# GNN kernel: counts added by two engines from bases in order of use, rank products and sums interleaved, first small loads issued by ScalarE

## The chip, the cores and the metric

The kernel runs on one core of one Trainium2 chip. The metric is the device time of one execution in microseconds (us), the median of several runs.

## What is computed

Two graph networks run one after the other on 3125 nodes with 128 features and 103125 edges, sorted by target node. The first is a four-layer GCN; the second has three relational layers over 16 edge types. For each (target, type) pair the second needs the number of edges, by which its sums are divided. Cut to that:

```python
seg = tgt * R + edge_type
agg = segment_sum(x[src], seg, N * R).reshape(N, R, d)
cnt = segment_sum(ones_like(edge_type), seg, N * R).reshape(N, R, 1)
out = einsum('nrd,rdo->no', agg / clip(cnt, 1.0), W_r) + x @ root_r + bias_r
```

## The kernel before, in words

The program is a row of stages. In each, every engine has a list of instructions written out by hand, ordered by semaphores, and a barrier of all engines ends it. A wait stands in front of one instruction; the instructions queued behind it on the engine wait too. Seven stages run in this order: `prepare`, `slots`, `count_relations`, `inverses_and_norm`, `build_adjacency`, `gcn_layers`, `relations`. The stages after the first two have a second, general form that runs only if the input breaks an assumption of the fast form (a flag decides); the inputs here take the fast form throughout.

`prepare` (from L217): SyncE (SP) issues 13 loads on one semaphore, `s_ld`: sources, targets and types of all edges (L230 to L232, 128x816 words each), the first target of each group of 512 edges (`gbase`, L233), and nine small ones (L235 to L237): three gains and three shifts of 256 words and three scalars, each broadcast to 128 partitions. VectorE and ScalarE wait for all 13. VectorE (L254 to L300) then forms `dloc`, the place of each edge's target within its group's window of 19 nodes; only L278 and L279 read the gains. A reciprocal (L300) ends it.

`slots` (from L1893): the rank of each edge among those of its group and block of sources. TensorE writes 24 sums into six PSUM banks in turn (L2028 to L2031), and VectorE picks from each: a product with a one-hot (L1972, 128x500 into one of two buffers `sized`) and a sum over blocks (L1974) that reads it. After the product stands a wait for its end and an `sem_inc` (L1973), which TensorE needs before it writes the bank again. 20 of the 24 steps are 500 wide, 4 are 25 wide.

`count_relations` (from L445): 202 groups of 512 edges, four at a time in 51 rounds. VectorE copies types and places to float16 (L485, L486), ScalarE fills the unused half of one one-hot (L517, eight instructions), VectorE makes the one-hots (L492 and L494, 70 instructions in two parts), and TensorE multiplies them (L533, four matmuls a round), which leaves a 128x76 result whose four diagonal blocks of 16x19 are the counts of four groups. Six rounds share a PSUM bank. VectorE then adds each block into `t.quarters` at the group's base node (L508): 202 additions of 16x19, one after another. The base comes from a register; 12 registers are loaded at a time (L499, the first 12 at L488), and each addition waits for the fourth one before it, which added to the same quarter of `t.quarters`. The first addition of every four has two waits, one for the bank (L505) and behind it the one for the fourth addition before (L507). The same form, two waits in a row ahead of one VectorE instruction, stands in the next stage at L630 and L631, ahead of L632. The four quarters are summed by a matmul in the next stage.

## Time and profile before

| | us |
|---|---|
| median of 3 runs | 3432.25 (3431.44 to 3438.33) |
| profiled execution | 3401.57 |
| its span | 3399.8 |
| TensorE busy | 2653.2 (78%) |
| VectorE busy | 2193.1 (65%) |
| ScalarE busy | 1323.8 (39%) |
| GpSimd busy | 1219.4 (36%) |

The profiled execution is 30.7 us shorter than the median of the unprofiled ones. Times in the rows are from the span's start, in us. In a row of the timeline, the start comes first, then the duration (of several instructions together where it ends in "x" and a number), then engine, line, operation, what is written and read; square brackets hold the idle time of the engine before it and what ended it. A "q" behind an engine's name means its sequencer.

### The profile page before, as it was taken

To read this page: it belongs to the slowest core of one execution; us is meant where nothing else is said; L and a number is where in the kernel's file an instruction comes from. 1 tells how busy PE (TensorE), PEld (TensorE's weight loads), DVE (VectorE), ACT (ScalarE), POOL (GpSimd) and SP (SyncE) were. 2 spreads that over 40 slices of the span, in tenths; PEclk is the share of its full clock that TensorE was granted. 3 is DMA by queue.
4 is the path that set the end of the run, shared out by engine and by line. 5 is a ranking of instruction groups with operands and counts; after the bars stand their busy time and mean duration, and the time that the engine had idled before them with its cause. 6 is when DMAs were issued, how large, how long until landed. Compare 5 with 4: busy or idle time off the path is not lost.

```text
span 3399.8 us, 80962 instructions
## 1 busy us (share of the span) xinstructions
PE 2653.2 (78%) x24551; PEld 1772.8 (52%) x24552; DVE 2193.1 (65%) x7930; ACT 1323.8 (39%) x2937; POOL 1219.4 (36%) x1269
## 2 busy tenths in 40 slices
PE   3337777768899995888888888888888888888887
PEld 1323333335456683555555555555555555555555
DVE  6689999976453454666566556656666556566665
ACT  0149999973222212333333333333333333333332
POOL 3020000000000002555555545555555455555554
PEclk9569999999999997999999999999999999999999
DMA  0011111121101026444444444444444444454442
GB/s 26 20 58 43 46 43 46 43 68 47 32 24 45 8 78 208 121 124 122 121 118 121 124 123 118 121 122 123 120 120 122 124 119 122 121 123 121 120 121 80
DMA packets 228329, 314.99 MB, mean 93 GB/s; under 512 B 41665, under 2 KB 201004, under 8 KB 227708
## 3 DMA queue, kind: packets, MB, share of 16 engines
q1 hardware_dynamic: 187548, 227.23, 24.9%
q0 software_dynamic: 40672, 86.39, 9.0%
q8 instruction: 58, 0.95, 0.1%
q14 instruction: 51, 0.42, 0.0%
HBM read 268.23 MB, written 45.23 MB: 92 GB/s over the span
## 4 chain that ended last, share of the span: by engine, by line
PE 25%; DMA 16%; issue 10%; POOL 3%; DVE 3%; another core or an unknown queue 3%; DVEq 0%; POOLq 0%; ACT 0%; SPq 0%; ACTq 0%
DMA arena<-pair,arena 15%; PE psum L2308 8%; PE psum L2321 7%; PE psum L2332 4%; PE psum L2285 4%; POOL arena L2218 3%; DVE arena L2501 1%; PE psum L2298 1%; DVE arena L2507 1%; DVE arena L2497 1%; DVE arena L2537 0%; DMA arena<-rows 0%; PE psum L2386 0%; DMA pair<-arena 0%
## 5 line engine op out<-in xcount | busy, mean ns | idle before, releaser
L2218 POOL DMA_INDIRECT arena<-pair,arena x1212 | 1161.1, 958 | 906.7 <-DMA h<-h 381.9
L2507 DVE SCALAR_TENSOR_TENSOR arena<-psum,arena,work 128x304 f32<-128x304 f32 x606 | 429.9, 710 | 718.7 <-DMA h<-h 469.5
L2442 ACT ACTIVATE arena<-psum 128x512 f16<-128x512 f32 x303 | 180.7, 597 | 1108.3 <-remote 763.1
L2321 PE MATMUL psum<-arena 128*128 128x304 f16 x3939 | 566.1, 293 | 18.9 <-issue 17.8
L2308 PE MATMUL psum<-arena 128*128 128x304 f16 x2424 | 370.6, 296 | 207.3 <-DMA arena<-pair,arena 162.2
L2501 DVE TENSOR_SCALAR arena<-arena 128x304 f16<-128x304 f16 x2121 | 483.1, 300 | 0.0
L2321 PEld LDWEIGHTS psum<-arena 128*128 128x128 f16 x3939 | 360.9, 98 | 193.5 <-issue 81.7
L2285 PE MATMUL psum<-arena 128*32 128x256 f16 x7272 | 367.1, 277 | 117.9 <-issue 109.1
L2439 ACT ACTIVATE arena<-psum 128x1024 f16<-128x1024 f32 x303 | 308.9, 1019 | 227.8 <-DMA h<-h 134.7
L2308 PEld LDWEIGHTS psum<-arena 128*128 128x128 f16 x2424 | 213.7, 98 | 346.7 <-issue 234.4
L2332 PE MATMUL psum<-arena 128*128 128x152 f32 (+1 forms) x2496 | 378.0, 297 | 6.5 <-DVE arena L2507 6.5
L1254 PE MATMUL psum<-arena,h 128*128 128x512 f16 x1250 | 346.6, 383 | 19.4 <-DMA h<-h 19.4
L2332 PEld LDWEIGHTS psum<-arena 128*128 128x128 f32 x2496 | 346.1, 194 | 20.6 <-DVE arena L2507 10.0
L2285 PEld LDWEIGHTS psum<-arena 128*32 128x32 f16 x7272 | 157.4, 95 | 282.2 <-issue 264.4
L2497 DVE TENSOR_SCALAR arena<-arena 128x304 f16<-128x304 f16 x1212 | 280.2, 295 | 27.3 <-ACT arena L2420 19.0
L1062 POOL DMA_DIRECT2D h<-h x9 | 8.3, 926 | 799.4 <-issue 538.6
L1255 PE MATMUL psum<-arena,h 128*128 128x128 f16 x1250 | 275.3, 220 | 0.0
L989 PE MATMUL psum<-h,work 128*128 128x512 f16 (+1 forms) x404 | 110.6, 356 | 145.8 <-DVE work L853 145.8
L931 ACT ACTIVATE work<-h 128x128 f16<-128x128 f16 x707 | 216.6, 395 | 0.1
L1254 PEld LDWEIGHTS psum<-arena,h 128*128 128x128 f16 x1250 | 123.3, 99 | 168.3 <-DMA h<-h 20.2
L2537 DVE TENSOR_TENSOR arena<-arena,psum 128x19 f32 x606 | 105.8, 175 | 98.2 <-PE psum L2332 16.3
L2445 ACT ACTIVATE arena<-psum 64x128 f16<-64x128 f32 x606 | 159.7, 264 | 7.4
(289 smaller groups left out, 3217.6 us busy)
## 6 DMA issues: line engine op xcount, KB each, us to landing
work<-inverse SPq DMA_DIRECT2D x606, 152.0 KB
arena<-pull SPq DMA_DIRECT2D x303, 224.0 KB
pull<-rows SPq DMA_DIRECT2D x101, 224.0 KB
arena<-pair,arena POOLq DMA_INDIRECT x1212
h<-work SPq DMA_DIRECT2D x8, 640.0 KB
h<-h POOLq DMA_DIRECT2D x8, 640.0 KB, 6.9
pair<-arena SPq DMA_DIRECT2D x12, 256.0 KB
x_pad<-arena SPq DMA_DIRECT2D x1, 1600.0 KB, 5.3
```

Of the source, the lines that this page charges most:

```text
L931: e.activation(t.away[:, k, :], t.iota_h[:, 0:P], ACT.Abs, bias=t.stage[:, par, 0, k:k + 1], scale=-1.0).then_inc(s_df, 1)
L1254: e.matmul(bank[:, at:at + 512], wt, adj[:, b, i * GN:i * GN + 512], start=a, stop=z)
L1255: m = e.matmul(bank[:, at + 512:at + GN], wt, adj[:, b, i * GN + 512:i * GN + GN], start=a, stop=z)
L2218: e.indirect_dma_start(out=t.msg[:, j, k].rearrange("p h f -> p (h f)"), out_offset=None, in_=d[f"pair_{l}"].rearrange("n h f -> n (h f)") ...
L2285: m = e.matmul(p.psum[CAP * (b % 4):CAP * (b % 4) + CAP, GATHER + c // 2, c % 2 * 2 * RF:(c % 2 + 1) * 2 * RF], t.pull[:, slot, b * CAP:(b ...
L2308: m = e.matmul(p.psum[:, 0, 0:KEYS], t.msg[:, j % TP, tile, half, :], t.oh[:, j % 2, tile, :], start=(tile == 0 and half == 0), stop=(tile ...
L2321: m = e.matmul(p.psum[:, 1, 0:KEYS], t.smsg[:, j % 2, tile, half, :], t.soh[:, j % 2, tile, :], start=(tile == 0 and half == 0), stop=(til ...
L2332: m = e.matmul(p.psum[:, OUT + h, 0:n], t.wr[:, r, :], t.agg[h][:, r, :, :].rearrange("p g w -> p (g w)")[:, 0:n], start=(r == 0), stop=(r ...
L2439: e.activation(t.smsg[:, q, 0:4].rearrange("p k h f -> p (k h f)"), p.psum[:, GATHER:GATHER + 2, :].rearrange("p b n -> p (b n)"), ACT.Cop ...
L2497: e.tensor_scalar(t.oh[:, j % 2, k, :], t.iota[:, 0:KEYS], t.keys[:, j * GT + k:j * GT + k + 1], None, ALU.is_equal).then_inc(s_oh, 1)
L2501: e.tensor_scalar(t.soh[:, j % 2, c, :], t.iota[:, 0:KEYS], t.skeys[:, at:at + 1], None, ALU.is_equal).then_inc(s_oh, 1)
L2507: e.scalar_tensor_tensor(t.agg[h % 2][:, :, k % BATCH, :], p.psum[:, k % 2, 0:KEYS].rearrange("p (r w) -> p r w", r=REL), t.back[:, l:l + ...
```

## The change

Three things are changed. In `prepare` ScalarE issues the nine small loads, on a semaphore of their own (`s_gn`); VectorE waits at its start for the other four only, and for the nine in front of L278. In `slots` the products and sums of successive steps are interleaved: product n+1 is issued ahead of sum n, with a wait for sum n-1, and the product itself counts up the semaphore for TensorE. In `count_relations` VectorE adds only the blocks of the first two quarters (102 of them); ScalarE copies the blocks of the other two from PSUM to SBUF as float16, one bank at a time (18 copies), and GpSimd adds those (100 additions). The bases are first put into `t.bases` in the order in which each engine uses them, by two copies. In the general forms, a buffer `nodes_0` takes the place of `rows_0`.

```diff
@@ -231,11 +231,8 @@
         e.dma_start(t.gbase, d["gbase"].partition_broadcast(P)).then_inc(s_ld, 16)
-        for k in range(3):
-            e.dma_start(t.gains[:, k], d[f"g{k}"].partition_broadcast(P)).then_inc(s_ld, 16)
-            e.dma_start(t.gains[:, 3 + k], d[f"beta{k}"].partition_broadcast(P)).then_inc(s_ld, 16)
-            e.dma_start(t.sig[:, k:k + 1], d[f"a{k}"].partition_broadcast(P)).then_inc(s_ld, 16)
-        e.wait_ge(s_ld, 13 * 16)
+        e.wait_ge(s_ld, 4 * 16)
+        e.wait_ge(s_gn, 9 * 16)
...
@@ -250,7 +247,7 @@
         v = Tally(p.sem("prep"))
-        e.wait_ge(s_ld, 13 * 16)
+        e.wait_ge(s_ld, 4 * 16)
         v.inc(e.tensor_copy(t.typf, t.typ))
...
@@ -275,6 +272,7 @@
                               ALU.subtract))
+        e.wait_ge(s_gn, 9 * 16)
         v.inc(e.tensor_reduce(t.red[:, 3:4], t.gains[:, 0:3], AX.XY, ALU.max, apply_absolute_value=True))
...
@@ -301,7 +299,11 @@
     def _(e):
-        e.wait_ge(s_ld, 13 * 16)
+        for k in range(3):
+            e.dma_start(t.gains[:, k], d[f"g{k}"].partition_broadcast(P)).then_inc(s_gn, 16)
+            e.dma_start(t.gains[:, 3 + k], d[f"beta{k}"].partition_broadcast(P)).then_inc(s_gn, 16)
+            e.dma_start(t.sig[:, k:k + 1], d[f"a{k}"].partition_broadcast(P)).then_inc(s_gn, 16)
+        e.wait_ge(s_gn, 9 * 16)
         e.wait_ge(s_sq, 1)
...
@@ -464,6 +468,12 @@
         return a.rearrange("p (m g k) -> p m g k", g=G, k=GT)
+
+    def load(e, regs, part, q):
+        first, stop = part * 2 * LOAD, min(GPAD, (part + 1) * 2 * LOAD)
+        if first < NG:
+            e.load(regs[part % 2][0:(stop - first) // 2],
+                   t.bases[0:1, q // 2 * (GPAD // 2) + first // 2:q // 2 * (GPAD // 2) + stop // 2])
...
@@ -478,6 +488,25 @@
         e.memset(t.x[:, BLOCKS - 1, :], 0.0).then_inc(s_tail, 1)
+        e.wait_ge(s_tail, 1)
+        regs = [[e.alloc_register(f"copy_base{q}_{k}") for k in range(LOAD)] for q in range(2)]
+        e.wait_ge(s_16, 4)
+        load(e, regs, 0, 2)
+        done = 0
+        for n in range(NG):
+            if n % (2 * LOAD) == 0:
+                load(e, regs, n // (2 * LOAD) + 1, 2)
+            m, q = n // G, n % G
+            if q < 2:
+                continue
+            base = e.snap(regs[n // (2 * LOAD) % 2][n % (2 * LOAD) // G * 2 + q - 2], min_val=0, max_val=NODES - 1)
+            to = t.quarters[32 * q:32 * q + REL, bass.ds(base, RWIN)]
+            if m % PER_BANK == 0:
+                e.wait_ge(s_cp, 2 * (m // PER_BANK) + q - 1)
+            if done > 1:
+                e.wait_ge(s_ag, done - 1)
+            e.tensor_tensor(to, to, t.copies[32 * q:32 * q + REL, m * RWIN:(m + 1) * RWIN], ALU.add).then_inc(s_ag, 1)
+            done += 1
...
@@ -485,28 +514,34 @@
         typ, dloc = (a.rearrange("p (g n) -> p g n", g=G) for a in (t.typ16, t.dloc16))
-        e.load(regs[0], t.gbase[0:1, 0:LOAD])
-        e.wait_ge(s_16, 2)
+        for h in range(2):
+            e.tensor_copy(t.bases[0:1, h * (GPAD // 2):(h + 1) * (GPAD // 2)].rearrange("p (m g) -> p m g", g=2),
+                          t.gbase[0:1, :].rearrange("p (m g) -> p m g", g=G)[:, :, 2 * h:2 * h + 2]).then_inc(s_16, 1)
+        e.wait_ge(s_16, 4)
+        load(e, regs, 0, 0)
         for a, z in PARTS:
             for r in range(REL):
                 e.tensor_scalar(t.hot_r[:, :, r, a:z], typ[:, :, a:z], float(r), None, ALU.is_equal)
             for w in range(RWIN):
                 one = e.tensor_scalar(t.hot_c[:, :, w, a:z], dloc[:, :, a:z], float(w), None, ALU.is_equal)
             one.then_inc(s_hot, 1)
+        done = 0
         for n in range(NG):
-            if n % LOAD == 0 and n + LOAD < NG:
-                more = min(LOAD, NG - n - LOAD)
-                e.load(regs[n // LOAD % 2 ^ 1][0:more], t.gbase[0:1, n + LOAD:n + LOAD + more])
+            if n % (2 * LOAD) == 0:
+                load(e, regs, n // (2 * LOAD) + 1, 0)
             m, q = n // G, n % G
+            if q > 1:
+                continue
             bank, at = place(m)
-            base = e.snap(regs[n // LOAD % 2][n % LOAD], min_val=0, max_val=NODES - 1)
+            base = e.snap(regs[n // (2 * LOAD) % 2][n % (2 * LOAD) // G * 2 + q], min_val=0, max_val=NODES - 1)
             to = t.quarters[32 * q:32 * q + REL, bass.ds(base, RWIN)]
             if q == 0:
                 e.wait_ge(s_mm, min(ROUNDS, (m // PER_BANK + 1) * PER_BANK))
-            if n >= G:
-                e.wait_ge(s_ad, n - G + 1)
+            if done > 1:
+                e.wait_ge(s_ad, done - 1)
             e.tensor_tensor(to, to, p.psum[32 * q:32 * q + REL, bank, at + q * RWIN:at + (q + 1) * RWIN],
                             ALU.add).then_inc(s_ad, 1)
+            done += 1
...
@@ -516,6 +551,13 @@
                              ACT.Copy).then_inc(s_rest, 1)
+        for h in range(BANKS):
+            m0, m1 = h * PER_BANK, min(NG // G, (h + 1) * PER_BANK)
+            e.wait_ge(s_mm, m1)
+            for q in (2, 3):
+                sums = p.psum[32 * q:32 * q + REL, h % 8, 0:(m1 - m0) * WIDE].rearrange("p (m w) -> p m w", w=WIDE)
+                e.activation(t.copies[32 * q:32 * q + REL, m0 * RWIN:m1 * RWIN].rearrange("p (m w) -> p m w", w=RWIN),
+                             sums[:, :, q * RWIN:(q + 1) * RWIN], ACT.Copy).then_inc(s_cp, 1)
...
@@ -528,7 +570,8 @@
             if m >= 8 * PER_BANK:
-                e.wait_ge(s_ad, PER_BANK * G)
+                e.wait_ge(s_ad, PER_BANK * 2)
+                e.wait_ge(s_cp, 2)
             for k in range(GT):
...
@@ -1198,7 +1241,7 @@
-                e.dma_start(d["rows_0"][:, cols].rearrange("p (b f) -> p b f", f=RF), ex).then_inc(s_st, 16)
+                e.dma_start(d["nodes_0"][rows].rearrange("(b p) f -> p b f", p=P), ex).then_inc(s_st, 16)
...
@@ -1658,7 +1701,7 @@
-        e.dma_start(t.hrows, d["rows_0"].rearrange("p (b f) -> p b f", f=RF)).then_inc(s_r, 16)
+        e.dma_start(t.hrows, d["nodes_0"].rearrange("(b p) f -> p b f", p=P)).then_inc(s_r, 16)
...
@@ -1699,7 +1742,7 @@
-                 out=t.msg[:, 0, :], out_offset=None, in_=p.d[f"rows_{l}"][:, :],
+                 out=t.msg[:, 0, :], out_offset=None, in_=p.d[f"rows_{l}" if l else "nodes_0"][:, :],
...
@@ -1963,16 +2006,29 @@
-        n = 0
-        for q, g0, g1 in SPREAD:
-            for k in range(GT):
-                e.wait_ge(s_rk, n + 1)
-                w = (g1 - g0) * BLOCKS
-                x = t.sized[n % 2][:, 0:w]
-                v.link(e, e.tensor_tensor(x, p.psum[:, n % 6, 0:w], flat(t.ohb[:, k, g0:g1, :]), ALU.mult))
-                e.sem_inc(s_used)
-                v.inc(e.tensor_reduce(grid(t.place)[:, g0:g1, k], x.rearrange("p (g b) -> p g b", b=BLOCKS), AX.X, ALU.add))
-                n += 1
+        steps = [(g0, g1, k) for q, g0, g1 in SPREAD for k in range(GT)]
+
+        def chosen(n):
+            g0, g1, k = steps[n]
+            w = (g1 - g0) * BLOCKS
+            e.wait_ge(s_rk, n + 1)
+            if n > 1:
+                e.wait_ge(s_sum, n - 1)
+            e.tensor_tensor(t.sized[n % 2][:, 0:w], p.psum[:, n % 6, 0:w], flat(t.ohb[:, k, g0:g1, :]),
+                            ALU.mult).then_inc(s_used, 1)
+
+        def summed(n):
+            g0, g1, k = steps[n]
+            e.wait_ge(s_used, n + 1)
+            e.tensor_reduce(grid(t.place)[:, g0:g1, k],
+                            t.sized[n % 2][:, 0:(g1 - g0) * BLOCKS].rearrange("p (g b) -> p g b", b=BLOCKS),
+                            AX.X, ALU.add).then_inc(s_sum, 1)
+
+        chosen(0)
+        for n in range(len(steps)):
+            if n + 1 < len(steps):
+                chosen(n + 1)
+            summed(n)
...
@@ -1983,6 +2039,7 @@
+        e.wait_ge(s_sum, len(steps))
...
@@ -2591,6 +2648,8 @@
+    t.copies = p.work[:, GPAD + NPAD + TPAD:GPAD + NPAD + TPAD + 25 * RWIN].bitcast(F16)
+    t.bases = p.work[:, GPAD + NPAD + TPAD + 25 * RWIN:2 * GPAD + NPAD + TPAD + 25 * RWIN].bitcast(I32)
...
@@ -2632,6 +2691,7 @@
+    make("nodes_0", (NPAD, RF), F32)
     make("table_0", (P, BLOCKS * 2 * RF), F16)
```

## Rows read from the trace of the kernel before

**Rows 1.** By stretch: busy us of PE, PEld, DVE, ACT, POOL; clock, DMA share, GB/s

```profile
103.00:138.00 35.00, 28.52 (x204) 28.17 (x204) 25.00 (x145) 10.84 (x8) 0.00 (x0) 0.50 0.16 46
138.00:177.00 39.00, 0.00 (x0) 0.00 (x0) 21.86 (x128) 0.00 (x0) 0.00 (x0) 0.50 0.00 1
```

**Rows 2.** Timeline of the count stage: matmuls, additions, and what follows

```profile
109.22 28.52 PE L533 MATMUL psum<-arena 128*128 128x76 f16 x204 [21.86 <-DVE arena L494]
...
115.30 2.39 DVE L508 TENSOR_TENSOR work<-work,psum 16x19 f32 x12
...
148.92 2.69 DVE L508 TENSOR_TENSOR work<-work,psum 16x19 f32 x12 [0.99 <-DVE work L508]
...
171.91 5.04 DVE L508 TENSOR_TENSOR work<-work,psum 16x19 f32 x22 [1.22 <-issue]
```

**Rows 3.** Sequencer instructions by line: duration ns min/median/max, first and last start

```profile
L499 DVEq TENSOR_LOAD <-work x16: 846/848/1086, 113.3 to 170.5; - x16
...
L507 DVEq EVENT_SEMAPHORE  x50: 21/21/21, 115.5 to 176.4; - x50
...
L631 DVEq EVENT_SEMAPHORE  x5: 21/21/21, 199.8 to 203.6; - x5
```

**Rows 4.** ScalarE in the count stage, and its smallest common copy from PSUM

```profile
102.09 11.75 ACT L517 ACTIVATE arena<-work 128x1600 f16<-128x1600 f16 x8 [77.23 <-DVE work L485]
...
L2445 ACT ACTIVATE arena<-psum 64x128 f16<-64x128 f32 x606 | 159.7, 264 | 7.4
```

**Rows 5.** GpSimd's instructions grouped by shape: busy us, mean ns of one | idle before

```profile
L2218 POOL DMA_INDIRECT arena<-pair,arena x1212 | 1161.1, 958 | 906.7 <-DMA h<-h 381.9 <-issue 325.9 <-PE psum L2321 149.5
...
L1914 POOL TENSOR_SCALAR_AFFINE_SELECT arena<-arena 125x125 f16<-125x125 f16 x2 | 0.6, 334 | 0.1
L1916 POOL TENSOR_SCALAR_AFFINE_SELECT arena<-arena 125x5 f16<-125x5 f16 x1 | 0.5, 504 | 0.0
...
L247 POOL TENSOR_SCALAR_AFFINE_SELECT ident<-ident 128x128 f32<-128x128 f32 x1 | 0.3, 292 | 0.2 <-POOL ident L245 0.2
...
L245 POOL MEMSET ident<- 128x128 f32 x1 | 0.2, 194 | 0.0
...
L2663 POOL MEMSET const-float32-1.0<- 128x1 f32 x1 | 0.1, 102 | 0.0
```

**Rows 6.** Timeline from 27 us: GpSimd beside a VectorE product of two SBUF inputs

```profile
27.34 11.16 DVE L1929 TENSOR_TENSOR arena<-arena 128x2525 f16<-128x2525 f32 x4 [1.99 <-issue]
...
30.25 2.83 POOL L1905 TENSOR_SCALAR_AFFINE_SELECT arena<-arena 125x125 f16<-125x125 f16 x1
```

**Rows 7.** Timeline of the first 25 us: issue of the loads, VectorE's work

```profile
2.21 0.43 SPq L233 DMA_DIRECT2D work<-in_gbase  x1
...
6.50 1.15 SPq L237 DMA_DIRECT2D arena<-in_a  x1
13.01 0.58 DVE L254 CAST arena<-arena 128x816 f32<-128x816 int32 x1 [12.89 <-DMA arena<-in_a]
...
20.41 0.95 DVE L278 TENSOR_REDUCE arena<-arena 128x1 f32<-128x768 f32 x1
```

**Rows 8.** DMA issues of the first 14 us, size, median us to landing

```profile
arena<-in_g SPq DMA_DIRECT2D x3, 128.0 KB, 6.4
...
work<-in_gbase SPq DMA_DIRECT2D x1, 102.0 KB, 4.4
```

**Rows 9.** Busy time by stretch in the first microseconds, columns as in rows 1

```profile
4.00:5.00 1.00, 0.00 (x0) 0.00 (x0) 0.00 (x0) 0.00 (x0) 0.00 (x0) 1.00 1.05 385
6.00:7.00 1.00, 0.00 (x0) 0.00 (x0) 0.00 (x0) 0.00 (x0) 0.00 (x0) 1.00 1.06 238
```

**Rows 10.** Timeline of VectorE in the rank steps: product, sum, next product

```profile
62.34 0.68 DVE L1972 TENSOR_TENSOR arena<-psum,arena 128x500 f32<-128x500 f32 x1
63.16 0.68 DVE L1974 TENSOR_REDUCE arena<-arena 128x20 f32<-128x500 f32 x1
63.75 0.67 DVE L1972 TENSOR_TENSOR arena<-psum,arena 128x500 f32<-128x500 f32 x1
```

6 lines of the change are left out of this document (4 added, 2 removed).

## The prediction

> **What bounds the kernel now.** The change touches the first 177 us of a span of 3399.8. I read the busy times by stretch first. From 138 to 177 us VectorE alone works, 21.86 us busy of 39; TensorE, ScalarE and GpSimd do nothing; while the matmuls run, GpSimd is idle too and TensorE's granted clock is 0.50, its lower level of 1.2 GHz [rows 1]. Then the timeline: the 204 matmuls are over 28.52 us after 109.22, but the 202 additions run from 115.30 to 176.95 [rows 2], and the barrier follows. So the additions set the end of this stage, with some 39 us in which nothing else runs. Twelve additions take 2.69 us and are followed by 0.99 us of idle time [rows 2]; what fills it is the load of 12 registers, 848 ns on VectorE's sequencer [rows 3]. In the first stage the timeline shows VectorE at rest until 13.01 us, released by the last small load, issued at 6.50; the last of the four large ones was issued at 2.21 [rows 7] and landed 4.4 us later [rows 8]. In the rank steps VectorE is never long idle: product at 62.34, sum at 63.16, next product at 63.75, thus 1.41 us a step [rows 10]. All three stages hang on VectorE, and a barrier ends each, so what they lose in length, the program loses. Later stages get the same work later or earlier as a whole.
>
> **First loads.** The nine small loads leave SP's queue and are issued by ScalarE, idle until then. By itself, `gbase` lands at 2.21 + 4.4 = 6.6 us [rows 7, 8], and VectorE could start at 6.8. But now the small loads (six of 128 KB, 0.77 MB) run beside the large ones. At 385 and 238 GB/s, what the DMA engines moved at 4 and 6 us [rows 9], all of it costs 2.0 to 3.2 us, none of it 0; I take half of it at 238 GB/s, 1.6 us, since ScalarE issues the last ones when the large ones have mostly landed. Start at 8.3, thus 13.01 - 8.3 = 4.7 us saved. Ends: 6.2 (start at 6.8) and 1.5 (start at 11.5, if the new queue slows the old one more than bytes explain; a small load now takes 6.4 us to land where 102 KB took 4.4 [rows 8]). The moved wait stands in front of L278, which VectorE reaches 20.41 - 13.01 = 7.4 us after its start [rows 7], at 15.7; even the landing of today, 13.0, is earlier, so it costs nothing.
>
> **Rank steps.** It looks as if two stalls a step were taken away. They are not. Product n+1 waits for sum n-1, and that sum stands directly ahead of it on the same queue; it must, since there are only two buffers. Before, the sum waited for the product just ahead of it; after, the product waits for the sum just ahead of it: one stall a step as before, 63.16 - (62.34 + 0.68) = 0.14 us [rows 10]. Its size stays as well. Today an `sem_inc` instruction stands in that gap. It goes, but the product has two waits now, and where an instruction has two waits, the trace shows the second as an instruction of its own: L631 is the second wait ahead of L632, and L507 shows one in front of every first addition of a four [rows 3]. The second wait is the one for the sum, so the same instruction fills the same gap. I take 0; the ends are 24 x 0.14 = 3.4 us gained if the gap goes altogether, and 24 x 0.02 (the 21 ns of one more sequencer instruction [rows 3]) = 0.5 us lost.
>
> **Start of the count stage.** Two copies of 102 bases are added, and the first load of registers, which ran beside L485, now waits for both and stands ahead of the one-hots. 0.2 us each for the copies, an estimate above the 0.17 of an addition [rows 2], plus 0.85 for the load [rows 3]: 1.25 us on VectorE, all of it in front of the one-hots. They, the matmuls and the additions move from 115.30 to 116.55.
>
> **VectorE's additions.** Two of four stay: 102. An addition takes 2.69/12 = 0.22 us [rows 2]; now every second one, not every fourth, has a second wait, so I take 0.25. Eight loads of registers stay of 16, at 0.92 us each (period of twelve, 2.69 + 0.99 = 3.68 [rows 2], less twelve starts 0.23 apart). 102 x 0.25 + 8 x 0.92 = 32.9: VectorE ends at 149.4. TensorE keeps ahead: a round takes 28.52/51 = 0.56 us [rows 2], two additions and their share of the loads 0.64.
>
> **GpSimd's additions.** They start when ScalarE is through L517, at 102.09 + 11.75 = 113.84 [rows 4], TensorE has filled the first bank (109.22 + 1.25 + 6 x 0.56 = 113.8) and two copies are made, at 0.264 us each as the nearest row [rows 4]: about 114.3. The copies of the later banks, 18 x 0.26 = 4.8 us in all, lie beside the matmuls on an engine that is idle. The price of one addition decides all; the trace has no two-input operation on GpSimd. Lower end: 0.10, a memset of one column. Upper end: 0.504, the dearest undisturbed select, 125x5. Between: a memset of 128x128 takes 0.194, the select that also reads it 0.292 [rows 5], so one read costs 0.10; a small memset and two reads give 0.10 + 2 x 0.10 = 0.30. I take 0.30. With eight loads of registers at VectorE's 0.92 (7.4 us; GpSimd has its own bases), it ends at 114.3 + 30 + 7.4 = 151.7. That is later than VectorE's 149.4, so GpSimd sets the end of the stage: 176.95 - 151.7 = 25.2 us saved. If it were cheaper, VectorE would be the bound: 27.5.
>
> The Trainium skill speaks against the move: its page GPSIMD Engine Reference, section Performance versus the Vector engine, has GpSimd at about half of VectorE's speed in two-input elementwise work. By it an addition would cost 2 x 0.17 = 0.34 (an estimate from that ratio), the stage would end at 155.7 and the kernel at 3406. No row here has such an operation on GpSimd.
>
> **Rest.** `nodes_0` is touched by the general forms only, which these inputs don't run: 0.
>
> **Sum.** 4.7 + 0 + 25.2 = 29.9 us (the 1.25 is within the 25.2). The profiled execution would go from 3401.57 to 3371.6. It lies 30.7 below the median of the runs; nothing in the change bears on that distance, so the median goes from 3432.25 to 3402.3.
>
> **Rivals.**
> (a) The two adders get in each other's way. For it: a select of 125x125 on GpSimd took 2.83 us beside VectorE products of 2.79 us with two SBUF inputs [rows 6], against 0.334 alone [rows 5]. Against it: VectorE's addition has one input in PSUM. The Trainium skill (SBUF — State Buffer, Who interferes with whom) names just this difference: it sees contention with two SBUF inputs, none with one; the first half agrees with the 2.83 us, the second is seen in no row. If they took turns, a pair would cost 0.17 + 0.30 = 0.47 on both: 116.55 + 102 x 0.47 + 7.4 = 171.9, 5.0 us saved there, 9.7 in all: 3422.5.
> (b) GpSimd is dear: each addition costs what its DMA instructions cost, 0.958 [rows 5], because each goes through software and waits for the end of the one before the last. It would end at 114.3 + 95.8 + 7.4 = 217.5, 40.6 later than now; less 4.7, the kernel is 35.9 slower: 3468. The sum is zero at (181.65 - 121.7)/100 = 0.60 us an addition and slower by more than 0.2% from 0.67. Against it: all plain GpSimd operations of small size undisturbed by VectorE are at or below 0.504 [rows 5].
> (c) GpSimd at 0.54 to 0.67 an addition: the gain of the loads and the loss of the additions cancel within 7 us: 3432.
> (d) The start does not do what it says: both queues slow each other, and VectorE starts at 11.5: 3405.5.
>
> **How the numbers follow.** Forecast (additions at 0.10 to 0.40, first load gain of 3 to 6) 0.64; (d) 0.09; (a) 0.16; (c) 0.05; (b) 0.06. What this kernel's measurement can tell from no change is about 0.2%, 6.9 us. The range: below, VectorE sets the end (27.5), start 6.2, rank gap gone 3.4: 3395, and 4 for the scatter of the runs: 3391. Above, an addition at 0.504 (end 172.1, 4.8 saved) with 1.5 at the start: 3426. It takes in the forecast, (d) and (a). Faster 0.89, same 0.05, slower 0.06.
>
> **What would show it.** In the profile after: first copy of VectorE at 7 to 9 us; in the rank steps still 1.4 us a step, with a gap now behind the sum and none behind the product; one-hots starting 1.2 us later in the stage; 102 additions on VectorE over 33 us; 100 on GpSimd with 0.3 from start to start, ending 2 us behind VectorE's. Wrong if GpSimd's additions are more than 0.45 apart, or VectorE's own get longer beside them, or the next stage's start does not move with the additions.

## The result and the profile after

| | before | after |
|---|---|---|
| median of 6 runs | 3433.16 (3431.44 to 3438.33) | 3420.65 (3418.87 to 3425.55) |
| ratio, 95% interval | | 0.9965 [0.9955, 0.9975] |
| profiled execution | 3401.57 | 3420.5 |
| its span | 3399.8 | 3418.8 |

The median of before is over three executions more than in the table ahead of the prediction. The change saves 12.5 us, by the interval 8.6 to 15.4. The forecast was 29.9 us. The direction held, and the time is inside the range; less than half of the gain arrived.

The two spans can't be compared as wholes. The last stage took 2097.0 us in the profiled execution of before and 2126.9 in that of after, although nothing in it was changed; in later profiles of kernels that leave it alone it took 1862 to 1879 us on some chips and 2125 to 2131 on others. So from here on stages are compared, from barrier to barrier. The first four lie ahead of everything that varies:

| stage, us | before | after | difference | forecast |
|---|---|---|---|---|
| first loads (`prepare`) | 26.2 | 23.7 | -2.5 | -4.7 |
| rank steps (`slots`) | 74.0 | 72.6 | -1.4 | 0 |
| counts (`count_relations`) | 77.9 | 64.5 | -13.4 | -25.2 |
| normalization (`inverses_and_norm`) | 30.7 | 38.3 | +7.6 | 0 |
| end of the four | 208.8 | 199.1 | -9.7 | -29.9 |

The next two stages are within 1.1 us of before. The two terms of the sum came in at about half of their size, and a stage that the change doesn't touch pays 7.6 us.

Read by stretch (columns as in [rows 1]; count stage and normalization of after), GpSimd now works 24 us of the count stage, and VectorE's busy time in the normalization stage is 31.5 us where it is 23.88 before:

```profile
96.30:160.80 64.50, 28.47 (x204) 28.13 (x204) 31.44 (x176) 16.24 (x26) 24.01 (x101) 0.50 0.10 26
160.80:199.10 38.30, 10.85 (x50) 10.74 (x50) 31.48 (x95) 5.21 (x7) 15.15 (x11) 0.50 0.33 103
```

TensorE's granted clock is 0.50 in both stages, its lower level of 1.2 GHz, as in [rows 1]; the clock plays no part in the difference.

The timeline of the count stage of after, which answers to [rows 2] (start, duration, engine, line):

```profile
98.96 0.40 DVE L518 COPY work<-work 1x102 int32<-1x102 int32 x2
102.24 2.86 DVE L524 TENSOR_SCALAR arena<-work 128x400 f16<-128x400 f16 x16 [2.88 <-issue]
...
112.48 5.45 POOL L508 TENSOR_TENSOR work<-work 16x19 f16 x12 [15.27 <-ACT work L559]
...
115.48 2.84 DVE L542 TENSOR_TENSOR work<-work,psum 16x19 f32 x12 [0.87 <-PE psum L576]
...
150.69 2.88 DVE L542 TENSOR_TENSOR work<-work,psum 16x19 f32 x12 [2.88 <-issue]
...
155.45 4.60 POOL L508 TENSOR_TENSOR work<-work 16x19 f16 x16 [1.26 <-issue]
```

and by line, sequencer instructions among them, for the loads of registers (which answer to the L499 of [rows 3]) and both kinds of additions:

```profile
L475 DVEq TENSOR_LOAD <-work x9: 1406/2723/2782, 99.4 to 153.4; - x9
L475 POOLq TENSOR_LOAD <-work x9: 1386/2706/2721, 99.5 to 153.8; - x9
...
L508 POOL TENSOR_TENSOR work<-work x100: 212/218/2209, 112.5 to 159.8; 16x19 f16 x100
...
L542 DVE TENSOR_TENSOR work<-work,psum x102: 160/166/171, 115.5 to 159.7; 16x19 f32 x102
```

The additions are what they were forecast to be: 0.218 us each on GpSimd, 0.293 from start to start (forecast 0.30); 0.166 on VectorE, 0.216 and 0.284 from start to start in turn, 0.26 in the mean (0.25). The loads are not. The same instruction with the same 12 registers takes 2.72 us where it took 0.848, on both engines. The gaps "2.88 <-issue" ahead of the one-hots and ahead of additions are these loads.

The normalization stage of after, VectorE and GpSimd:

```profile
167.08 11.04 POOL L610 MEMSET arena<- 128x1600 f32 x8
...
169.70 8.46 DVE L654 TENSOR_SCALAR arena<-arena 128x25 f32<-128x25 f32 x1
178.19 0.18 DVE L656 TENSOR_SCALAR arena<-psum 128x25 f32<-128x25 f32 x1
```

In the kernel before, the same instruction (there L611), on the same data, among the same eleven memsets:

```profile
183.05 12.45 POOL L567 MEMSET arena<- 128x1600 f32 x9
...
187.04 0.22 DVE L611 TENSOR_SCALAR arena<-arena 128x25 f32<-128x25 f32 x1
190.28 0.18 DVE L613 TENSOR_SCALAR arena<-psum 128x25 f32<-128x25 f32 x1 [3.01 <-PE psum L649]
```

VectorE would have waited 3.0 us for TensorE there in any case, so an instruction of 8.46 us instead of 0.22 delays what follows by 8.24 - 3.0 = 5.2 us, of which experiments 6 to 8 find 4.6 at the stage's end. That is not all of the 7.6: the rest is at the end of the stage. VectorE's last branch there, and the DRAIN behind it:

```profile
L169 DVEq COMPARE_BRANCH  x1: 69/69/69, 194.0 to 194.0; - x1
...
L173 DVEq DRAIN  x1: 41/41/41, 198.2 to 198.2; - x1
```

Between the two lie 4.08 us in which VectorE does nothing; before, the same two stand at 206.7 and 207.3, and SP came to the barrier last, at 207.9. Here SP came at 195.2 and VectorE last.

In the first stage, the two queues issue side by side (answers to [rows 7]):

```profile
1.75 0.43 SPq L232 DMA_DIRECT2D arena<-in_typ_pt  x1
...
2.19 1.55 ACTq L303 DMA_DIRECT2D arena<-in_g  x1
2.23 1.54 SPq L233 DMA_DIRECT2D work<-in_gbase  x1
...
10.44 0.58 DVE L251 CAST arena<-arena 128x816 f32<-128x816 int32 x1 [10.31 <-DMA work<-in_gbase]
```

### The profile page after: what moved, and what is told of

Same layout as the page of the kernel before. It is cut to its first block, busy times and chain, and to the rows that moved or that the text cites. A ratio compares the mean times of both kernels' runs of the same rounds, so it can differ in the third digit from the quotient of the medians.

```text
span 3418.8 us, 81004 instructions
## 1 busy us (share of the span) xinstructions
PE 2676.5 (78%) x24551; PEld 1778.2 (52%) x24552; DVE 2179.1 (64%) x7832; ACT 1328.0 (39%) x2955; POOL 1247.5 (36%) x1369
## 4 chain that ended last, share of the span: by engine, by line
PE 28%; DMA 11%; issue 10%; DVE 5%; another core or an unknown queue 4%; POOL 2%; DVEq 0%; ACT 0%; POOLq 0%; SPq 0%; ACTq 0%
DMA arena<-pair,arena 11%; PE psum L2378 8%; PE psum L2365 8%; PE psum L2389 5%; PE psum L2342 5%; DVE arena L2558 2%; POOL arena L2275 2%; PE psum L2355 1%; DVE arena L2554 1%; DVE arena L2564 1%; DVE arena L2594 0%; DMA arena<-rows 0%; PE psum L2443 0%; DVEq L2594 0%
## 5 line engine op out<-in xcount | busy, mean ns | idle before, releaser
L2342 PE MATMUL psum<-arena 128*32 128x256 f16 x7272 | 400.8, 277 | 199.3 <-issue 186.5
L2342 PEld LDWEIGHTS psum<-arena 128*32 128x32 f16 x7272 | 166.3, 94 | 390.2 <-issue 368.2
L2389 PEld LDWEIGHTS psum<-arena 128*128 128x128 f32 x2496 | 341.4, 191 | 13.9 <-DVE arena L2564 3.1
```

The costliest lines, as they stand in the source:

```text
L2342: m = e.matmul(p.psum[CAP * (b % 4):CAP * (b % 4) + CAP, GATHER + c // 2, c % 2 * 2 * RF:(c % 2 + 1) * 2 * RF], t.pull[:, slot, b * CAP:(b ...
L2389: m = e.matmul(p.psum[:, OUT + h, 0:n], t.wr[:, r, :], t.agg[h][:, r, :, :].rearrange("p g w -> p (g w)")[:, 0:n], start=(r == 0), stop=(r ...
```

## The experiments

Ratios are to the kernel before on the same chip. Some chips take some 250 us less for the last stage, so times of different experiments aren't compared with each other. Where only one execution was made, the reading rests on the lengths of stages, and no ratio is given: where nothing in them was changed, the slots, count and normalization stages repeat within 0.2 us from chip to chip, the first stage within 1 us. Line numbers in a fence are those of the kernel it is of.

**1. Where the bases lie: `start_aligned`.** The copied bases started at word 4695 of `work` (a word is 4 bytes), those for GpSimd at 4797; the original bases, read in 0.848 us, at word 0. One edit moves the start to 4696:

```diff
-    t.bases = p.work[:, GPAD + NPAD + TPAD + 25 * RWIN:2 * GPAD + NPAD + TPAD + 25 * RWIN].bitcast(I32)
+    t.bases = p.work[:, GPAD + NPAD + TPAD + 476:2 * GPAD + NPAD + TPAD + 476].bitcast(I32)
```

> The changed kernel, with the array of bases moved by one word, from word 4695 to 4696 of the scratch row; its second half, read by GpSimd, stays 102 words on, at 4798. Theory (where the words lie): a load of 12 registers takes four adjacent words in one read where they start at a multiple of four, and one word a read otherwise. VectorE's loads (4696 + 12k, multiples of four) fall from 2.72 to 0.85 us; GpSimd's (4798 + 12k, never) stay at 2.7. VectorE's additions then end about 8 x 1.87 = 14 us earlier, but GpSimd's still end the stage, so the kernel gains at most the 1.9 us of the first load ahead of the one-hots. Rival (two engines loading at once, or words just written by a copy, make loads slow): both stay at 2.7 us, as the same engines load the same copied words.

Measured, loads by line:

```profile
L475 DVEq TENSOR_LOAD <-work x9: 834/848/868, 99.6 to 139.4; - x9
L475 POOLq TENSOR_LOAD <-work x9: 1390/2708/2758, 99.6 to 152.2; - x9
```

VectorE's half, now at a multiple of four words, is fast; GpSimd's, at 4798, is slow. VectorE's additions end at 145.3, GpSimd's at 158.5, and the stage is 62.7 us long instead of 64.5: GpSimd alone holds its end.

**2. Both halves at a multiple of four: `both_aligned`.**

```diff
-                   t.bases[0:1, q // 2 * (GPAD // 2) + first // 2:q // 2 * (GPAD // 2) + stop // 2])
+                   t.bases[0:1, q // 2 * 104 + first // 2:q // 2 * 104 + stop // 2])
```

(and the copies and the tile's size to match).

> As the kernel before this one, and the second half too starts at a multiple of four (word 4800, halves 104 apart). Theory of the words' place: loads of both engines at 0.75 to 0.85 us; VectorE's additions span 31 us instead of 44.4, GpSimd's 34 to 35 instead of 47.6, the one-hots start 1.9 earlier, the count stage lasts 64.5 - 15 = 49 to 50 us, and the kernel gains 14 to 16 us on the changed one: about 3405. Rival theory: no change, 3420.

Measured: 3155.31 (3145.71 to 3161.09), before 3183.98 on that chip; ratio 0.9916 [0.9903, 0.9929], where the change alone gave 0.9965. Loads and additions:

```profile
L475 DVEq TENSOR_LOAD <-work x9: 834/850/867, 99.5 to 139.4; - x9
L475 POOLq TENSOR_LOAD <-work x9: 795/808/835, 99.6 to 140.6; - x9
...
141.72 4.60 POOL L508 TENSOR_TENSOR work<-work 16x19 f16 x16 [0.67 <-POOL work L508]
```

The count stage takes 50.6 us, 13.9 less than in after and 27.3 less than before. VectorE's 102 additions take 32.5 us from first to last (forecast 32.9), GpSimd's 100 take 35.6 (forecast 37.4), and GpSimd ends 1.1 us behind VectorE (0.2 us in after). With fast loads the forecast for this stage would have been too low by 2 us and not too high by 12.

**3. The same without the rest of the change: `odd_before` and `even_before`.** The kernel before, its bases copied to word 4695 (odd), or to 4694 (even, but no multiple of four), and loaded from there:

```diff
-        e.load(regs[0], t.gbase[0:1, 0:LOAD])
-        e.wait_ge(s_16, 2)
+        e.tensor_copy(t.odd[0:1, :], t.gbase[0:1, :]).then_inc(s_16, 1)
+        e.wait_ge(s_16, 3)
+        e.load(regs[0], t.odd[0:1, 0:LOAD])
```

> The kernel before, with one added copy of the 204 bases to an odd word (4695) and the registers loaded from there; all 202 additions stay on VectorE, GpSimd adds nothing. Theory of the words' place: all 17 loads at 2.7 us instead of 0.85; 16 of them between additions, 16 x 1.87 = 30 us longer, and 2.3 more for the copy and the first load ahead of the one-hots: about 32 us slower than the kernel before. Rival (two engines loading at once): loads stay at 0.85, at most 1.3 us slower.

> The kernel before with its 204 bases copied to a word that is even but no multiple of four (4694), from where the registers are loaded, 12 at a time. The bases' own place is a multiple of four words (a load of 12 takes 0.85 us), the copy to 4695 took 2.73 us a load. Theory (only a start at a multiple of four words, 16 bytes, is fast): 2.7 us a load, count stage 109.6 as with the odd word. Rival (a multiple of two words, 8 bytes, is enough, or gives half): 0.85 to 1.6 us a load, count stage 78.5 to 91.

Measured from the odd word:

```profile
L500 DVEq TENSOR_LOAD <-work x16: 2285/2722/2727, 116.4 to 201.2; - x16
```

From the even word the median is 2722 ns as well. Both are slow, and the count stage takes 109.6 us in both. `odd_before` is 28.6 us slower than before, ratio 1.0091 [1.0076, 1.0106] (3212.62 us). So neither the second engine nor the interleaved order of the bases matters; the place does, and a multiple of two words isn't enough. The count stage lost 31.7 us, and the whole 28.6, with an interval of 24 to 34. What a load costs per register: 2.72/12 = 0.227 us from an unfit place, and 1.406/6 = 0.234 for the last, short one; 0.848/12 = 0.071 from a fit one. This looks like one read of 0.23 to 0.28 us for each four registers in the one case and for each register in the other; the 10 registers of before's last load, from a fit place, took 1.086 [rows 3], which two reads of four and two single ones would give (four reads at 0.27). The last load of `both_aligned` on VectorE, 6 registers from a fit place, took 0.834: as long as 12, as one read of four and two single ones would. A load with 4 or 8 registers was not run. And the place isn't all there is: the load of one register that begins each later stage, always from the same word, took 0.31 us in most stages, 0.55 at 26.3 and 0.94 at 208.9 in before. What sets that, no run shows.

**4. The first loads: `prepare_alone` and `prepare_one_queue`.** The first puts the change's own first part into the kernel before. The second leaves the issues where they were, on SP behind the large ones, and moves only the semaphore and the wait:

```diff
-            e.dma_start(t.gains[:, k], d[f"g{k}"].partition_broadcast(P)).then_inc(s_ld, 16)
+            e.dma_start(t.gains[:, k], d[f"g{k}"].partition_broadcast(P)).then_inc(s_gn, 16)
...
-        e.wait_ge(s_ld, 13 * 16)
+        e.wait_ge(s_ld, 4 * 16)
+        e.wait_ge(s_gn, 9 * 16)
```

> The kernel before with the first-stage part of the change alone: ScalarE issues the nine small loads. The prediction's step: first copy of VectorE at 8.3, 4.7 us earlier. What the changed kernel's profile says: 10.4, 2.6 earlier, since the two queues' issues slow each other. Expected: first copy at 10.4 +- 0.2, the issues of SP at 1.0 to 1.6 us each instead of 0.43, first stage 23.7 us instead of 26.2, later stages as before, normalization at 30.7.

> The kernel before with the small loads still issued by SP behind the four large ones, but counted on a semaphore of their own, so that VectorE waits for the four large ones alone and for the small ones only where it reads them (the wait ahead of L278). No second queue issues. Theory (what cost 2.1 of the forecast 4.7 us is the second queue's issuing, not its bytes): SP's issues stay at 0.43, gbase is issued at 2.2 and lands at 6.6, first copy at 6.8 to 7.5; the small loads land at 13.0 as before, ahead of the wait at some 14.5, so the first stage is 5.5 to 6 us shorter than before (20.3 to 20.8). Rival (the small loads' bytes behind the large ones delay them): first copy at 9 or later.

Measured for `prepare_alone`: first copy at 10.19, stage 23.4 us, the others as before. The expectation of 1.0 to 1.6 us for every issue of SP was wrong: only the last of its four is slow, 1.52 us, the three ahead of it took 0.42 to 0.43. For `prepare_one_queue`, the timeline:

```profile
2.21 0.43 SPq L233 DMA_DIRECT2D work<-in_gbase  x1
...
6.57 1.35 SPq L237 DMA_DIRECT2D arena<-in_a  x1
6.97 0.58 DVE L255 CAST arena<-arena 128x816 f32<-128x816 int32 x1 [6.85 <-DMA work<-in_gbase]
```

First copy at 6.97, stage 20.2 us: 6.0 less than before, without a second queue. The times from issue to landing (median) tell where the changed kernel loses it. First its rows, then those of `prepare_one_queue`:

```profile
arena<-in_src_pt SPq DMA_DIRECT2D x1, 408.0 KB, 5.1
...
work<-in_gbase SPq DMA_DIRECT2D x1, 102.0 KB, 8.2
```

```profile
arena<-in_src_pt SPq DMA_DIRECT2D x1, 408.0 KB, 3.3
...
work<-in_gbase SPq DMA_DIRECT2D x1, 102.0 KB, 4.7
```

With the second queue the base loads need 8.2 us instead of 4.7, 3.5 more, of which 1.54 - 0.43 = 1.1 is the issue itself and 2.4 comes after it. Already the very first load, issued at 0.8 us beside ScalarE's first, lands 1.8 us later. So the theory of the expectation (issuing, not bytes) covers a third. The larger part comes in the transfers; that the large and the small ones now share the DMA engines from the start would explain it, but no run separates this from other effects of the second queue. With one queue the small ones follow, and nothing waits for them: they had landed when SP's wait ended at 12.84, and VectorE is at the place that needs them some 14 us into the stage.

**5. The stall of the rank steps: `rank_three_buffers`.** The kernel before with the change's interleaving and three buffers:

```diff
-    t.sized = [c(ACROSS * BLOCKS) for _ in range(2)]
+    t.sized = [c(ACROSS * BLOCKS) for _ in range(3)]
...
+            if n > 2:
+                e.wait_ge(s_sum, n - 2)
```

> The kernel before with the interleaved rank steps of the change, but with three buffers for the products in turn instead of two, and the product waiting for the sum but two ahead of it. The prediction's step: with two buffers one stall a step is left, because the product waits for the sum that stands directly ahead of it. With three, both waits are for instructions that lie one instruction back. Expected: 0.14 to 0.2 us a step less than before (1.41), period 1.2 to 1.27, the slots stage 3.5 to 5 us shorter than the 74.0 of before, where two buffers gave 1.4. Rival (the step is bound by the two engines' work, 0.68 + 0.59, and not by the stall): period 1.36 as with two buffers.

Measured: the slots stage takes 68.3 us, 5.7 less than before. The timeline, first of after (two buffers), then of this kernel:

```profile
61.73 0.68 DVE L2017 TENSOR_TENSOR arena<-psum,arena 128x500 f32<-128x500 f32 x1
62.32 0.67 DVE L2023 TENSOR_REDUCE arena<-arena 128x20 f32<-128x500 f32 x1
63.09 0.68 DVE L2017 TENSOR_TENSOR arena<-psum,arena 128x500 f32<-128x500 f32 x1
```

```profile
63.48 0.66 DVE L1980 TENSOR_REDUCE arena<-arena 128x20 f32<-128x500 f32 x1
64.06 0.67 DVE L1974 TENSOR_TENSOR arena<-psum,arena 128x500 f32<-128x500 f32 x1
64.64 0.66 DVE L1980 TENSOR_REDUCE arena<-arena 128x20 f32<-128x500 f32 x1
```

A step takes 63.09 - 61.73 = 1.36 us with two buffers and 64.64 - 63.48 = 1.16 with three. With three, each instruction starts 0.58 us after the one before it, although each takes 0.67: where the next one doesn't wait for the end of the last, the two overlap by 0.09. So a wait for the instruction directly ahead costs the gap of 0.10 and this overlap, about 0.2 a step.

**6. VectorE held by the memsets: `no_port_wait`, `held_later`.** The first writes the same value with another instruction:

```diff
-        v.inc(e.tensor_scalar(n.value[:, BLOCKS:], n.mv[:, :, 1], EPS, None, ALU.add))
+        v.inc(e.scalar_tensor_tensor(n.value[:, BLOCKS:], n.mv[:, :, 1], EPS, n.mv[:, :, 1], ALU.add, ALU.max))
```

> The changed kernel, in which the one VectorE instruction in the next stage that took 8.46 us beside GpSimd's memsets (var + eps as a tensor_scalar) is a scalar_tensor_tensor with the same result, max(var + eps, var), from two SBUF inputs. Theory (a form of VectorE instruction that takes the SBUF interface shared with GpSimd was held until GpSimd's row of memsets was over): the new form is not held, takes 0.2 us, the stage lasts 30.4 us instead of 38.1, and the kernel gains 7.6 us: about 3413. Rival (any VectorE instruction is held there, or the unprofiled runs have no such hold): no gain in the runs.

Measured: 3168.21 (3164.67 to 3172.9), ratio 0.9952 [0.994, 0.9964]; normalization stage 33.5 us. Timeline:

```profile
169.83 0.19 DVE L654 SCALAR_TENSOR_TENSOR arena<-arena 128x25 f32<-128x25 f32 x1
173.06 0.18 DVE L656 TENSOR_SCALAR arena<-psum 128x25 f32<-128x25 f32 x1 [3.05 <-PE psum L692]
```

Nothing is held; 4.8 of the 7.6 us come back and 2.8 do not. The second puts five small instructions of this kind ahead of the TENSOR_SCALAR, which stays:

```diff
+        for k in range(5):
+            e.wait_ge(v.sem, v.n)
+            v.inc(e.scalar_tensor_tensor(n.tmp[:, 5 * k:5 * k + 5], n.mv[:, 0:5, 1], EPS, n.mv[:, 0:5, 1], ALU.add, ALU.max))
```

> The changed kernel with five small scalar_tensor_tensor instructions (into a scratch tile) ahead of the TENSOR_SCALAR of the variances, which starts some 0.7 to 1 us later by them. In the changed kernel it starts at 169.70, 0.13 us before the next of GpSimd's eleven memsets starts, and takes 8.46 us, until the last memset ends; in the kernel before it stands at the same distance and takes 0.22. Theory (VectorE's instruction is held whenever it meets GpSimd's row of queued memsets, until the row ends): it now takes 7.5 to 7.8 us and still ends at 178.1. Rival (it is a tie of one moment, at which the next memset gets ahead of VectorE; elsewhere it is held for the memset that runs at most): it takes 0.2 to 1.4 us and the normalization stage is 33.5 to 35 us instead of 38.3.

Measured:

```profile
170.78 7.49 DVE L657 TENSOR_SCALAR arena<-arena 128x25 f32<-128x25 f32 x1
178.30 0.18 DVE L659 TENSOR_SCALAR arena<-psum 128x25 f32<-128x25 f32 x1
```

1.08 us later it is held 0.97 less and ends at the same place, when the last of the eleven memsets ends. The rival, a tie of one moment, falls. That the five instructions ahead of it were not held beside the same memsets agrees with `no_port_wait`.

**7. What brings the hold about: `one_add_before`, `one_load_before`.** The hold came with every kernel that had the new count stage and this TENSOR_SCALAR, and with none that had the old stage. In the kernel before, one addition on GpSimd is put into the count stage, for nothing, or else one load of 12 registers:

```diff
+        e.memset(t.other, 0.0).then_inc(s_one, 1)
+        e.wait_ge(s_one, 1)
+        e.tensor_tensor(t.other[:, 0:RWIN], t.other[:, RWIN:2 * RWIN], t.other[:, 0:RWIN], ALU.add).then_inc(s_one, 1)
```

> The kernel before with one two-input addition on GpSimd (16x19, SBUF only, into a scratch tile, behind a memset of it) at the start of the count stage, where GpSimd is idle for the rest of the stage. In all kernels with the changed count stage, GpSimd's eleven memsets of the next stage have a step of 1.367 us at first, last 1.42 from the third on, and VectorE's TENSOR_SCALAR is held until the last of them ends (8.46 us; started 1.08 later it was held 7.49 and ended at the same memset). In all kernels with the count stage of before, the memsets' step is 1.374, and the same TENSOR_SCALAR takes 0.22. Theory (GpSimd keeps what its additions left it in, and so takes the port for a whole row): with one such addition the hold appears, 8.4 us, and the normalization stage takes 35 us instead of 30.7. Rival (it is the moment at which the stage starts, or something else in the count stage): 0.22 us, 30.7.

> The kernel before with one load of 12 registers on GpSimd in the count stage and no addition there. Theory of the addition: no hold, TENSOR_SCALAR 0.22 us, normalization stage 30.7. Rival (reading registers from SBUF is what changes GpSimd's memsets): hold of 8.4 us, stage 35.

Measured with the addition:

```profile
101.20 0.21 POOL L484 TENSOR_TENSOR work<-work 16x19 f32<-16x19 f32 x1
```

```profile
180.19 15.17 POOL L572 MEMSET arena<- 128x1600 f32 x11 [78.78 <-DVE arena L614]
```

```profile
186.93 8.47 DVE L616 TENSOR_SCALAR arena<-arena 128x25 f32<-128x25 f32 x1
```

One addition of 0.21 us at 101.20, in another stage and 85 us before, and VectorE is held for 8.47 us; the normalization stage takes 35.3 us instead of 30.7. With the register load it takes 30.7, and the TENSOR_SCALAR 0.22.

**8. What ends it: `select_after_adds`, `iota_after_adds`.** The changed kernel, with one instruction of another kind behind GpSimd's last addition. The first (its scratch tile left out):

```diff
+        e.wait_ge(s_ag, done)
+        e.memset(t.other, 0.0).then_inc(s_ag, 1)
+        e.wait_ge(s_ag, done + 1)
+        e.affine_select(out=t.other, in_=t.other, compare_op=ALU.not_equal, fill=1.0, base=0, pattern=[[-1, RWIN]],
+                        channel_multiplier=1).then_inc(s_ag, 1)
```

> The changed kernel with a memset and a select of 128x19 on GpSimd behind its last addition (scratch tile), some 0.5 us in the count stage. One addition on GpSimd, 80 us earlier and in another stage, was enough to have VectorE's TENSOR_SCALAR held for the rest of the row of memsets. In the kernel before, GpSimd ran only iotas, selects and memsets before that place, and nothing was held. Theory (the last instruction of another kind decides how GpSimd's memsets go): behind a select they go as before, the memsets' step is 1.374 from the first on, TENSOR_SCALAR takes 0.2, the normalization stage 33.5 to 34 us (the 3 us at the branch are left). Rival (one addition changes it for good): 8.46 us, 38.3.

> The same with an iota of 128x19 in place of memset and select. Theory as for the select if any instruction but a memset restores the old behaviour: TENSOR_SCALAR 0.2 us, normalization stage 33.5 to 34. Rival (only a select does, or nothing): 8.46 us, 38.3.

Measured with the select, which took 0.20 us at 161.01:

```profile
170.86 0.22 DVE L659 TENSOR_SCALAR arena<-arena 128x25 f32<-128x25 f32 x1
174.09 0.18 DVE L661 TENSOR_SCALAR arena<-psum 128x25 f32<-128x25 f32 x1 [3.01 <-PE psum L697]
```

The hold is gone; with the iota as well (0.222 us). The normalization stage takes 33.7 us in both. So it hangs on which instruction GpSimd ran last, memsets not counted: behind an addition its row of memsets keeps VectorE out to the end, behind a select or an iota it lets VectorE in between two of them. It shows in the memsets too: here and in before the one that VectorE cut in front of takes 1.46 us and the others 1.43; in after none takes longer than 1.43. What in GpSimd differs, no trace shows.

**9. The branch: `code_shifted`.** 64 short memsets and a wait at the head of VectorE's part of the first stage of the changed kernel, where VectorE idles until 10.4 us:

```diff
         v = Tally(p.sem("prep"))
+        for k in range(64):
+            v.inc(e.memset(t.dloc[:, k:k + 1], 1.0))
+        e.wait_ge(v.sem, v.n)
```

> The changed kernel with 64 short memsets (into t.dloc, which is written again later) at the head of VectorE's part of the first stage, where it idles until 10.4 us anyway. It moves all of VectorE's later code by 65 instructions, and nothing else. In the changed kernel VectorE's last instruction of the normalization stage, the branch over the general form (L169) at 194.03, is followed by 4.08 us of nothing, with a block of instructions of 8192 bytes fetched at 196.32 inside it; before, the same gap is 0.47. Theory (the target of the branch is no longer among the instructions at hand, because VectorE's program has become some 300 instructions shorter): with the code moved by half a block the gap is 0.5 and the normalization stage goes from 38.3 to about 34.8 us, or the gap appears behind another branch. Rival (VectorE waits there for something of the stage's work, a store or GpSimd): the gap stays at 4 us, wherever the code lies.

Measured:

```profile
L169 DVEq COMPARE_BRANCH  x1: 69/69/69, 194.1 to 194.1; - x1
...
L173 DVEq DRAIN  x1: 69/69/69, 194.7 to 194.7; - x1
```

The gap is 0.47 us, as before, and the stage takes 35.3 us instead of 38.3; that is 3.0 and not 3.6 less, since SP now comes to the barrier last, at 195.3. Where the code lies decides. Not all of it reaches the end of the kernel: the next stage, `build_adjacency`, took 543.9 us here and 542.9 in after, and 543.3 to 544.9 in all ten profiles without the long gap against 542.3 to 543.4 in the seven with it, 1.3 us in the mean. The packets of an instruction queue fit this. In after, between 194 and 199 us:

```profile
q14 instruction: 2, 0.02, 0.8%
```

that is two blocks of 8192 bytes, of which one starts at 196.32, behind the branch; in `code_shifted` the last one ahead of the branch starts at 185.33, none between it and the DRAIN, and the next at 196.35, behind the barrier. VectorE executes 306 instructions fewer than before up to there, so it looks as if the target of this branch, which skips the general form of the stage, came to lie in a block that isn't fetched yet; for which engine a block is fetched, the profile doesn't say. The Trainium skill (Runtime: NRT & Kernel Launch, Instruction fetch mechanics) describes just this: instructions come in blocks in straight order, and a taken branch out of the blocks at hand stalls for a fetch. The trace agrees, with a block fetched inside a gap of 4.08 us.

**10. All of it together: `all_mended`.** The edits of 2, 4 (one queue), 5, 6 (other instruction) and 9 in the changed kernel, and the first register load behind the one-hots instead of ahead of them.

> The changed kernel with each place mended that the runs so far point to: small loads issued by SP behind the large ones but counted by themselves; three product buffers in the rank steps; the bases copied to words that are a multiple of four, for both halves; the first load of registers behind the one-hots; the variance's addition written as scalar_tensor_tensor (max of var + eps and var, the same value); and VectorE's code moved by 65 instructions with short memsets at its head. Theory (each cause stands by itself, so the stages add up as they did alone): first stage 20.2 to 20.5, slots 68.3, counts 49.5 to 50.6, normalization 30.4 to 31, in all 169 to 171 us instead of 208.8, thus 38 to 40 us and a ratio of 0.9875 +- 0.002. Rival (a later wait takes over in one of them, as the norm stage did in the changed kernel): one of the four stages is more than 1.5 us above these numbers.

Measured: 3132.81 (3131.66 to 3134.46), before 3172.9 on that chip; ratio 0.9872 [0.985, 0.9893], 40.1 us less than before. By stretch (first stage, slots, counts, normalization):

```profile
0.00:21.20 21.20, 0.20 (x2) 0.10 (x3) 12.55 (x96) 1.49 (x2) 1.87 (x8) 1.00 0.35 102
21.20:89.50 68.30, 30.25 (x175) 16.63 (x175) 56.09 (x100) 0.00 (x0) 24.87 (x22) 0.91 0.00 0
89.50:139.30 49.80, 28.47 (x204) 28.13 (x204) 31.38 (x176) 16.26 (x26) 23.44 (x101) 0.50 0.12 34
139.30:170.00 30.70, 10.85 (x50) 10.74 (x50) 23.82 (x95) 5.21 (x7) 15.16 (x11) 0.50 0.36 114
```

170.0 us where before needs 208.8: 38.8 less. Each stage is as long as the mended causes make it one by one, but for two: the first takes 21.2 instead of 20.2, as `gbase` landed 5.7 us after its issue in this execution, not 4.7, and the counts take 49.8 instead of 50.6, with the first load behind the one-hots.

## Why the prediction was right or wrong

**Count stage, the failed step: "Eight loads of registers stay of 16, at 0.92 us each" and, for the first one, "0.85 for the load".** The price was read from the row of the old load [rows 3] and carried to loads from another place, whose address nobody looked at. They took 2.72 us. The copies sit at word 4695, behind a tile of 25 x 19 words. That costs 1.9 us ahead of the one-hots (they start 3.2 us later in the stage, forecast 1.25) and 1.9 for each further load of 12 on GpSimd: 64.5 - 50.6 = 13.9 us in all, by `both_aligned`. This term alone takes the forecast gain from 29.9 to 16.0 us. What else there is in the stage was 2.1 us dearer in the forecast (77.9 - 25.2 = 52.7) than in `both_aligned` (50.6). The Trainium skill (Runtime: NRT & Kernel Launch, Instruction fetch mechanics) gives about 200 ns per register for a load of registers, even in bulk; it speaks of loads from HBM, and these come from SBUF. The 0.227 us from an unfit place are near that figure, the 0.071 from a multiple of four words are not, and the measurement decides.

**Additions: right.** 0.293 a step on GpSimd against 0.30; VectorE 102 in 32.5 us against 32.9; GpSimd ends last, by 1.1 us with fast loads and by 0.2 in after, where the forecast had 2.3. Rival (a), that they take turns, falls: VectorE's additions take 0.166 us each beside GpSimd's, no more than the 0.17 of the forecast. But GpSimd's first addition took 2.209 us, beside VectorE's last one-hots, and the others follow it one by one without a wait for data. These 2.0 us are on GpSimd's path; without them VectorE would end last, so they cost the stage 0.2 us in after and 1.1 in `both_aligned` (estimates from the two ends). The prediction had no such term. Rivals (b) and (c) fall with 0.218 us an addition.

**Rank steps: right in kind.** The forecast was "one stall a step as before", with 3.4 us and -0.5 as ends, and 0 taken. Measured are 1.4 us, from a gap of 0.10 instead of 0.14. The stall is there, between sum and product, with the second wait as an instruction of its own, as forecast; `rank_three_buffers` shows that it is due to the two buffers. Its real worth, 5.7 us, is above the end of 3.4 that the prediction gave for the gap, since the overlap of two instructions wasn't counted.

**First loads: the right mechanism, sized too small.** "I take half of it at 238 GB/s, 1.6 us": the two queues together cost 3.5 us (10.44 against 6.97), 1.1 at the issue and 2.4 in the transfers. The start at 10.4 lies between the forecast's 8.3 and the 11.5 of rival (d). That 6.8 is possible with the small loads behind the others was in the text as the lower end; the change could have had it by moving only the wait.

**Normalization: a step that the prediction didn't have.** It had later stages "later or earlier as a whole", and its last part asked only for the next stage's start. The start did move; the stage's length changed, by 4.6 us through the state in which additions leave GpSimd, and by 3.0 through the place of the code. Neither could be read from the rows of before: no GpSimd addition stands in them, and a new place for the code is not worked out in any view. The Trainium skill (SBUF — State Buffer, Who interferes with whom) says that GpSimd keeps the shared ports for the whole of one instruction. By that VectorE would wait for at most one memset, 1.43 us; the trace shows 8.46, and the measurement decides. That a change which shortens VectorE's program by 300 instructions shifts every later branch could have stood in the text as a bound of some us to both sides.

**The account.** Forecast -29.9; register loads +13.9, the rest of the count stage -2.1, first loads +2.2, rank steps -1.4, hold +4.6, branch +3.0, sum -9.7, as the first four stages have it. `build_adjacency` is 1.1 us shorter (see experiment 9), and `gcn_layers` 0.1, which makes -10.9; the runs have -12.5 [-15.4, -8.6].

The time lies inside the range of 3391 to 3426 by luck: the upper end was made for a GpSimd addition of 0.504 us and a start at 11.5, and neither came. For the profiled execution 3371.6 was forecast and 3420.5 measured. Of that distance 29.9 us are the last stage, which the change doesn't touch, so "nothing in the change bears on that distance" held for the median and not for the single execution.

## What to carry to other kernels

Ask of each moved buffer where it begins, before its readers are priced: a load of 12 registers took 0.85 us or 2.72 by that alone. When work is given to an engine that was idle, look at the next stages too, at what the engine does there beside others, and at the length of the code: what was saved in one stage was partly paid in the next one. And try the smallest form of an edit first: moving the wait without the nine issues gave 6.0 us, with them 2.5; a third buffer gave 5.7, the interleaving with two 1.4.

## What the runs showed of the hardware that was not expected

- A load of registers from SBUF: 0.848 us for 12 from a multiple of four words; 2.72 from an odd word and from an even one that is no multiple of four; on GpSimd 0.81 and 2.71.
- One GpSimd TENSOR_TENSOR of 0.21 us changes how later memsets of GpSimd treat VectorE: TENSOR_SCALAR 128x25 took 8.47 us 85 us later, 0.22 without it, 0.22 again behind one select or iota. SCALAR_TENSOR_TENSOR at the same place took 0.19 (it was run behind additions only).
- Behind a branch VectorE did nothing for 4.08 us instead of 0.47, with the fetch of a block of instructions in between, and 65 harmless instructions far ahead of it took that away; 3.0 us of it came back in that stage, and the next one was 1.0 us longer.
- Two queues that issue at once: the fourth DMA issue of each took 1.54 us instead of 0.43, and a load of 408 KB landed 5.1 us after its issue instead of 3.3.
- Two dependent VectorE instructions of 0.67 us started 0.77 apart (wait for the one directly ahead), independent ones 0.58.
